# Gated cross-attention and low-rank expert layer on one core: turning tiles by VectorE blocks and SBUF moves in place of TensorE transposes

## The chip, the cores and the metric

One core of one Trainium2 chip runs the whole layer in one launch. The metric is the device time of that launch in microseconds (us), lower is better. Engine names as in the profile: PE is TensorE, DVE VectorE, ACT ScalarE, POOL GpSimd, SP SyncE (here it only waits and issues DMAs).

## The reference, cut to what matters

```python
# x, ctx: (16, 128, 1024) f32; attention: 8 heads of 64 over 128 channels; experts: 64 of rank 16, top 16
def xattn(q, k, v, Wq, Wk, Wv, Wo, bo, g):
    qh = einsum('bcn,oc->bon', q, Wq)            # likewise kh, vh, split into heads
    qh = softmax(qh, axis=-2) * SCALE            # over the 64 channels of a head
    kh = softmax(kh, axis=-1)                    # over the 1024 positions
    context = einsum('bhdn,bhen->bhde', kh, vh)
    out = einsum('bhde,bhdn->bhen', context, qh) # then Wo, + bo
    return out / norm(out, axis=1) * g * sqrt(128)
def ffn(x, A, B, Wr):
    scores = xf @ Wr.T                           # 64 scores a token, softmax over the top 16
    h = einsum('nd,krd->nkr', xf, A)             # 64 x 16 = 1024 hidden values a token
    return einsum('nkr,kdr->nd', h * G, B) * 2
x = x + tanh(g_xattn) * xattn(layernorm(x), ctx, ctx, ...)
x = x + tanh(g_ffn) * ffn(layernorm(x), A, B, Wr)
```

## The kernel before

**Arithmetic.** Every large product is made of three float32r passes (`three_pass`, lines 59 to 63): high part by high part, low by high, high by low. So each operand is kept as a pair: ACT copies it to float32r (the `hi_...` functions), and DVE or POOL subtracts that copy from the source (the `lo_...` functions).

**Stage one** (16 batch elements, bodies 0 to 15 and a tail body, `body(b, head, tail, ahead)` on each engine) is software-pipelined by hand: body b works on the keys and queries of element b and on the context and the output of element b-1. Keys: `mm_k(b, j)` makes key block j of four (128 key channels by 1024 positions) in the PSUM pair `psK`; DVE takes the maximum (`max_k`), ACT the exponential into `ek[:, j % 2]` (`exp_k`); PE turns it in eight 128x128 transposes into `psT` (`tr_k`, line 1298), ACT and DVE take the pair `ekT` from there (`hi_k` line 635, `lo_k` line 916). `psK` is single: `mm_k(b, j)` waits for `exp_k(b, j-1)`. `context(b)` (24 matmuls) needs all of `ekT` of element b, and runs at the start of body b+1. Queries go a similar way through `mm_q`, `max_q`, `shift_q` (subtracts the maximum by a matmul), `exp_q`, `tr_q` (line 1307), `hi_q`, `lo_q` and `output`. `psT` is handed from one turning to the next (`free_T`). DVE also has the layer norm of the next element (`stats`, `std`), and in bodies 2 to 4 one more reduction of 1024 elements, `part_early` (line 851). Each result of the attention goes to DRAM (`u_scratch`).

**Stage two** (`ffn_body`, b = 1 to 15): element b is normalised into `y` (the buffer `u_in`), turned by PE into `psY` (`tr_y`, line 1373, eight transposes), split by `hi_y` and `lo_y` into `yT`; `up(b, p)` multiplies by the router and A in three pieces (448, 384, 256 columns, 8 chunks of 3 passes each); DVE finds the top 16 (`route`) and gates the hidden values into `hg` (`gated`, line 1023); PE turns `hg` in two groups of four transposes (`tr_h`, line 1402), `hi_h` and `lo_h` split them into `hT`, and `down` multiplies by B (48 matmuls of 512 columns). DVE's `result` adds the residual. Beside that run the steps that prepare element b+2 and b+3: the load of u, `square_u`, `part_u`, `sum_u` (PE, line 1361), `norm_u` with `spread` (line 885), `residual` (POOL), `stats2`, `normalise`. The order on PE in a body:

```python
up(b, 0); tr_h(b - 1, 1); up(b, 1); up(b, 2); sum_u(b + 2)
tr_y(b + 1, j % 2); down(b - 1, 0); tr_h(b, 0); down(b - 1, 1)
```

What orders all this is the written order on each engine and the semaphores; nothing is planned by a scheduler. SP's order in a body of stage two is: store the result of b-2, load x of b+2, load u of b+3.

Of the kernel before, what the change touches and what calls it, by code (L numbers as in the profile page):

```python
# [6 lines left out]
def flamingo_layer(nc, x, ctx, ctxT, g_xattn, g_ffn, WqT, WkT, Wv, WoT, bo, g, AT, BT, u_dram, out):  # L7
# [9 lines left out]
    P = 128  # L17
# [70 lines left out]
    with outer:  # L88
# [8 lines left out]
        def at(kb, name, shape, dt=f32):  # L97
# [39 lines left out]
        ekT = [at(80, "ekT_hi", [P, BK, HD], f32r), at(96, "ekT_lo", [P, BK, HD], f32r)]  # L137
# [22 lines left out]
        yT = [at(152, "yT_hi", [P, DC, P], f32r), at(68, "yT_lo", [P, DC, P], f32r)]  # L160
        u_first = at(192, "u_first", [P, N])
# [7 lines left out]
        hT = [at(176, "hT_hi", [P, KC, P], f32r), at(180, "hT_lo", [P, KC, P], f32r)]  # L169
        hg = at(184, "hg", [P, KR])  # L170
# [12 lines left out]
        psN_early, psN = ps[:, 7, 0:EARLY * (N // 32)], ps[:, 4, 256:256 + N // 32]  # L183
# [14 lines left out]
            sem("k_mm"), sem("k_max"), sem("k_exp"), sem("k_T"), sem("k_hi"), sem("k_lo"), sem("k_rec"))  # L198
        q_mm, q_max, q_shift, q_exp, q_half, q_sum, q_rec, q_norm, q_T, q_hi, q_lo = (
# [50 lines left out]
        def _(sp):  # L250
# [52 lines left out]
            load_x(0, 0)  # L303
            sp.wait_ge(u_done, 1)
# [46 lines left out]
        def _(pool):  # L351
# [34 lines left out]

            def halve(b, p):
# [20 lines left out]
            def lo_a(t):  # L408
                pool.wait_ge(a_loaded, 16 * DC)
# [66 lines left out]
            def body(b, head, tail, ahead, split=False):  # L476
# [88 lines left out]
        def _(act):  # L565
# [32 lines left out]
            def exp_k(b, j):  # L598
# [977 lines left out]
```

## Time and profile before

| | |
|---|---|
| three runs | 959.32, 960.50, 960.53 us; median 960.5 |
| profiled execution | 959.67 us, of which its span is 957.9 us; granted TensorE clock 0.994 |
| PE | busy 932.2 us, 97% of the span, 5084 matmuls and transposes |
| PE weight load | busy 800.5 us |
| DVE, ACT, POOL | busy 704.0 (73%), 492.2 (51%), 469.5 us (49%) |
| chain that ended last | PE 81%, DVE 10%, issue 5% |
| stage one, stage two | to about 541 us; from about 550 us |

How to read it: the span is what the trace covers, and the rest of the execution (1.8 us) lies around it. Matmuls are pipelined, so a busy PE need not be PE at its peak: what one matmul costs is the distance of its start to the next start, which the chain that ended last gives. The share of a wait in that chain, not an engine's idle time, says what a shorter operation can give.

### The profile page before, as it was taken

The page shows a single profiled execution, that of the slowest core. Times are in us where ns is not written, and L with a number is a line of the kernel's source. Part 1 is how long each engine was busy: PE and PEld are TensorE (multiplying, and loading weights), DVE is VectorE, ACT ScalarE, POOL GpSimd, SP SyncE. Part 2 cuts the span into 40 slices and gives each one's busy share as a digit, 9 for nine tenths or more (in the row PEclk, how much of TensorE's full clock was granted, in tenths as well). Part 3 has the DMA queues.
Part 4 walks back from the last instruction along what each step waited for, and adds up shares of the span by engine and source line. Part 5 has one row for each costly group of instructions (what it writes and reads, how often), then busy time and mean ns, then how long its engine had stood idle before and what let it go on. Part 6 is the DMA issues. An engine that isn't in the chain of part 4 may idle for free.

```text
span 957.9 us, 16074 instructions
## 1 busy us (share of the span) xinstructions
PE 932.2 (97%) x5084; PEld 800.5 (84%) x5084; DVE 704.0 (73%) x1532; ACT 492.2 (51%) x974; POOL 469.5 (49%) x323
## 2 busy tenths in 40 slices
PE   7899999999999999999999799999999999999998
PEld 5687887888888888888888699999999999999986
DVE  6888888888888888888888857766666666666521
ACT  4687786678768767876787634222222222222100
POOL 3775657678777877785787824222222111111100
PEclk9999999999999999999999999999999999999999
DMA  4226231231323113311312853121111111111001
GB/s 153 89 66 249 93 104 49 89 133 66 109 91 133 66 68 132 109 68 66 131 45 88 300 199 128 67 67 67 66 67 67 66 66 66 66 66 45 23 23 44
DMA packets 24805, 88.31 MB, mean 92 GB/s; under 512 B 3264, under 2 KB 3264, under 8 KB 24768
## 3 DMA queue, kind: packets, MB, share of 16 engines
q1 hardware_dynamic: 19296, 67.91, 19.9%
q0 software_dynamic: 5184, 19.40, 6.1%
q10 hardware_dynamic: 288, 0.52, 0.2%
q8 instruction: 21, 0.34, 0.1%
q14 instruction: 16, 0.13, 0.0%
HBM read 71.04 MB, written 16.78 MB: 92 GB/s over the span
## 4 chain that ended last, share of the span: by engine, by line
PE 81%; DVE 10%; issue 5%; ACT 1%; POOL 1%; DMA 1%; DVEq 0%; ACTq 0%; POOLq 0%
PE ps L61 22%; PE ps L63 22%; PE ps L62 22%; PE ps L1307 6%; PE ps L1298 4%; DVE qT_lo L909 3%; PE ps L1288 2%; PE ps L1402 1%; PE ps L1373 1%; DVE mt L933 1%; DVE ekT_lo L916 1%; DVE qmax L895 1%; DVE bn L831 1%; DVE kmax L889 1%; DVE qsum L900 1%
## 5 line engine op out<-in xcount | busy, mean ns | idle before, releaser
L471 POOL TENSOR_TENSOR rb<-u_in,rb 128x1024 f32<-128x1024 f32 x14 | 33.7, 2408 | 255.4 <-DVE rb L885 255.4
L400 POOL TENSOR_TENSOR qe<-qe,qrec 128x1024 f32<-128x1024 f32 x64 | 121.2, 1903 | 47.1 <-DVE qrec L903 47.1
L61 PE MATMUL ps<-aT_hi,yT_hi 128*128 128x448 f32 (+2 forms) x384 | 128.4, 334 | 5.4 <-issue 5.4
L63 PE MATMUL ps<-aT_lo,yT_hi 128*128 128x448 f32 (+2 forms) x384 | 126.6, 330 | 0.0
L62 PE MATMUL ps<-aT_hi,yT_lo 128*128 128x448 f32 (+2 forms) x384 | 126.5, 330 | 0.0
L909 DVE TENSOR_TENSOR qT_lo<-ps,qT_hi 128x512 fp32r<-128x512 f32 x128 | 82.4, 686 | 49.0 <-ACT qT_hi L628 48.5
L393 POOL TENSOR_TENSOR qhalf<-qe 128x512 f32<-128x512 f32 x64 | 82.2, 1284 | 64.8 <-ACT qe L620 61.8
L61 PE MATMUL ps<-bT_hi,hT_hi 128*128 128x512 f32 x256 | 102.6, 401 | 0.0
L63 PE MATMUL ps<-bT_lo,hT_hi 128*128 128x512 f32 x256 | 100.0, 391 | 0.0
L62 PE MATMUL ps<-bT_hi,hT_lo 128*128 128x512 f32 x256 | 99.8, 390 | 0.0
L700 ACT ACTIVATE hT_hi<-ps 128x512 fp32r<-128x512 f32 x32 | 19.1, 597 | 143.8 <-PE ps L1402 143.8
L635 ACT ACTIVATE ekT_hi<-ps 128x512 fp32r<-128x512 f32 x128 | 70.1, 607 | 32.9 <-PE ps L1298 32.5
L916 DVE TENSOR_TENSOR ekT_lo<-ps,ekT_hi 128x512 fp32r<-128x512 f32 x128 | 81.2, 676 | 1.0 <-ACT ekT_hi L635 1.0
L889 DVE TENSOR_REDUCE kmax<-ps 128x1 f32<-128x1024 f32 x64 | 77.6, 1213 | 3.4 <-PE ps L63 1.9
L61 PEld LDWEIGHTS ps<-aT_hi,yT_hi 128*128 128x128 f32 x384 | 73.1, 190 | 8.0 <-issue 5.6
L604 ACT ACTIVATE ek<-ps,kmax 128x1024 f32<-128x1024 f32 x64 | 72.3, 1130 | 13.4 <-DVE kmax L889 13.4
L628 ACT ACTIVATE qT_hi<-ps 128x512 fp32r<-128x512 f32 x128 | 69.5, 599 | 14.4 <-PE ps L1307 14.4
L62 PEld LDWEIGHTS ps<-aT_hi,yT_lo 128*128 128x128 f32 x384 | 73.2, 191 | 2.3
L63 PEld LDWEIGHTS ps<-aT_lo,yT_hi 128*128 128x128 f32 x384 | 73.0, 190 | 2.0
L613 ACT ACTIVATE qe<-ps 128x1024 f32<-128x1024 f32 x48 | 49.3, 1027 | 47.8 <-PE ps L1288 47.7
L1307 PEld LDWEIGHTS ps<-ident,qe 128*128 128x128 f32 x512 | 57.9, 140 | 17.7 <-issue 8.5
L1307 PE MATMUL ps<-ident,qe 128*128 128x128 f32 x512 | 68.8, 276 | 3.8 <-DVE ekT_lo L916 3.5
(155 smaller groups left out, 2397.5 us busy)
## 6 DMA issues: line engine op xcount, KB each, us to landing
x_in<-in_x SPq DMA_DIRECT2D x16, 512.0 KB, 4.4
ctx_in<-in_ctx SPq DMA_DIRECT2D x16, 512.0 KB, 4.9
ctxT_in<-in_ctxT SPq DMA_DIRECT2D x16, 512.0 KB, 3.4
ctxT_hi<-in_ctxT POOLq DMA_DIRECT2D x16, 512.0 KB, 3.8
u_scratch<-osb SPq DMA_DIRECT2D x16, 512.0 KB, 3.8
out<-res SPq DMA_DIRECT2D x16, 512.0 KB, 2.8
x<-in_x SPq DMA_DIRECT2D x15, 512.0 KB, 4.0
u_in<-u_scratch SPq DMA_DIRECT2D x14, 512.0 KB, 3.2
```

What stands on the lines that cost most here:

```text
L61: nc.tensor.matmul(psum, whi, mhi, start=start, stop=False)
L62: nc.tensor.matmul(psum, wlo, mhi, start=False, stop=False)
L63: return nc.tensor.matmul(psum, whi, mlo, start=False, stop=stop)
L393: nc.gpsimd.tensor_tensor(qhalf[:, p % 2, :].rearrange("p (h d) -> p h d", d=DH // 2), v[:, :, 0:DH // 2], v[:, :, DH // 2:DH], ALU.add).t ...
L400: nc.gpsimd.tensor_tensor(v, v, w, ALU.mult).then_inc(q_norm, 1)
L604: nc.scalar.activation(ek[:, j % 2, :].rearrange("p (a n) -> p a n", a=HF), psK, ACT.Exp, bias=kmax[:, j:j + 1], accum_out=ksum[:, j:j + 1 ...
L628: nc.scalar.activation(qT[0][:, :, n * P:n * P + P], psT[:, h, :].rearrange("p (j n) -> p j n", n=P), ACT.Copy).then_inc(q_hi, 1)
L635: nc.scalar.activation(ekT[0][:, 4 * h:4 * h + 4, j * P:j * P + P], psT[:, h, :].rearrange("p (n d) -> p n d", d=P), ACT.Copy).then_inc(k_ ...
L889: nc.vector.tensor_reduce(kmax[:, j:j + 1], psK, axis=AX.XY, op=ALU.max, negate=True).then_inc(k_max, 1)
L909: nc.vector.tensor_tensor(qT[1][:, :, v], psT[:, h, :].rearrange("p (j n) -> p j n", n=P), qT[0][:, :, v].bitcast(f32), ALU.subtract).then ...
L916: nc.vector.tensor_tensor(ekT[1][:, n, w], psT[:, h, :].rearrange("p (n d) -> p n d", d=P), ekT[0][:, n, w].bitcast(f32), ALU.subtract).th ...
L1307: last = nc.tensor.transpose(psT[:, h, j * P:j * P + P], qe[:, p, w:w + P], ident[:, :])
```

## The change

Three of the turnings lose their TensorE transposes: those of `y` for elements 2 to 15, those of `hg` for all elements, and those of key block 0 of stage one. In their place DVE transposes the tile in place in blocks of 32x32 (`turn_y`, `turn_h`, `turn_k`), and SP moves the blocks between partition groups with 16 DMAs of 32 partitions by 256 columns each (32 KB) from SBUF to SBUF (`move_turned`). ACT and DVE (for keys ACT and POOL, `lo_moved_k`) then split the moved tile as a whole, 1024 columns at a time, from SBUF and not from PSUM. Key block 0 is moved into `ekT_raw[0]`, which lies on the low half of `ekT`, so its move waits for the context of the element before. The rows of A and B are laid out in another order on the host, to fit the order in which the strips land. `down` is one run of 48 matmuls. TensorE still turns key blocks 1 to 3, all of the queries, and `y` of elements 0 and 1.

```diff
+        MOVED = 16 * (P // 32) ** 2
+        def move_turned(queue, dst, src, s, slot=None):
+            for a in range(P // 32):
+                for q in range(P // 32):
+                    rows, cols = slice(32 * a, 32 * a + 32), slice(256 * q, 256 * q + 256)
+                    queue.dma_start(dst[32 * q:32 * q + 32, 256 * a:256 * a + 256],
+                                    src[rows, cols] if slot is None else src[rows, slot, cols]).then_inc(s, 16)
...
@@ SP @@
+            def move_k(b, j):
+                if j == 0 and started(b):
+                    wait_apart(sp, sp_turns, (kc_mm, b))
+                wait_apart(sp, sp_turns, (k_turned, turned_before(b, j) + 1))
+                move_turned(sp, ekT_raw[j], ek, k_moved[j], j % 2)
...
                     load(ctx_in[:, :], ctx, b + 1, ctx_loaded)
+                    for j in TURNED:
+                        move_k(b, j)
...
+            sp.wait_ge(h_turned, 1)
+            sp.wait_ge(o_mm, 2 * NB)
+            move_turned(sp, h_raw, hg, h_moved)
             def ffn_body(i, j):
...
+                if not isinstance(i, int) or b <= NB - 2:
+                    sp.wait_ge(y_turned, b)
+                    move_turned(sp, y_raw, y[(j + 2) % 2], y_moved)
                 if not isinstance(i, int) or b <= NB - 4:
-                    sp.wait_ge(y_T, 2 * b + 4)
+                    sp.wait_ge(y_moved, MOVED * b)
                     load_u(b + 3, j % 2)
+                sp.wait_ge(h_turned, b + 1)
+                move_turned(sp, h_raw, hg, h_moved)
@@ POOL, body @@
+            def lo_moved_k(b, j):
+                pool.wait_ge(k_hi, 8 * b + 2 * j + 2)
+                hi, lo = (t[:, 4 * j:4 * j + 4, :, :].rearrange("p g n i -> p (g n i)") for t in ekT)
+                nc.gpsimd.tensor_tensor(lo, ekT_raw[j][:, :], hi.bitcast(f32), ALU.subtract).then_inc(k_lo_pool, 1)
...
+                if head:
+                    lo_moved_k(b, 0)
                 if isinstance(b, int) and b == NB - 2:
                     early_newton()
@@ ACT, body @@
                 if head:
-                    hi_k(b, 0)
+                    hi_moved_k(b, 0)
+                if tail and head:
+                    hi_q(b - 1, 2)
+                if head:
                     exp_k(b, 2)
                     exp_q(b, 1)
-                if tail and head:
-                    hi_q(b - 1, 2)
@@ ACT, ffn_body @@
+                if not first:
+                    hi_moved_h(b - 1)
                 if not isinstance(i, int) or b <= NB - 2:
                     normalise(b + 1, (j + 2) % SLOTS)
-                hi_h(b - 1, 1)
+                if first:
+                    hi_moved_h(0)
                 exp_scores(b)
                 if not isinstance(i, int) or b <= NB - 2:
-                    hi_y(b + 1)
-                hi_h(b, 0)
+                    hi_moved_y(b + 1)
@@ DVE, body @@
                 if tail:
                     sum_q(b - 1, 2)
+                if head:
+                    turn_k(b, 0)
...
                     max_q(b, 1)
                     max_k(b, 2)
-                    lo_k(b, 0)
@@ DVE, ffn_body @@
+                if not first:
                     result(b - 2, (j + 1) % 2, (j + 3) % SLOTS, 2 * i + (j - 1) // 2)
-                if not isinstance(i, int) or b <= NB - 3:
+                    lo_moved_h(b - 1)
+                if norms:
                     part_u(b + 2)
+                if ahead:
+                    turn_y(b + 1, j % 2)
                 route(b)
-                if isinstance(i, int) and b == 1:
+                if first:
                     lo_b(4)
                     lo_b(6)
-                lo_h(b - 1, 1)
+                    lo_moved_h(0)
+                elif norms:
                     norm_u(b + 2)
                 for p in range(len(PIECES)):
                     gated(b, p)
-                    lo_y(b + 1)
-                lo_h(b, 0)
-                if not isinstance(i, int) or b <= NB - 3:
+                turn_h(b)
+                if ahead:
+                    lo_moved_y(b + 1)
+                if norms:
                     stats2(b + 2, (j + 3) % SLOTS)
@@ PE, body @@
                     mm_q(b, 1)
                     mm_k(b, 2)
-                    tr_k(b, 0, next(turn))
                 if tail and head:
+                    tr_q(b - 1, 2, next(turn))
                     output(b - 1, 0, range(CH // 2))
@@ PE, ffn_body @@
                 up(b, 0)
-                if isinstance(i, int) and b == 1:
-                    tr_h(0, 0)
-                else:
-                    tr_h(b - 1, 1)
+                if norms and not first:
+                    sum_u(b + 2)
                 up(b, 1)
                 up(b, 2)
-                    tr_y(b + 1, j % 2)
-                down(b - 1, 0)
-                tr_h(b, 0)
-                down(b - 1, 1)
+                down(b - 1)
```

`gated` now waits for the move of `hg` (`h_moved`) where it waited for `tr_h`, and `hi_moved_y` for the end of `up(b, 2)`, since `yT` is single. `context` waits for three blocks from DVE and one from POOL.

The order on SP's queue in one body of the loop of stage two, before (lines of the kernel before):

```order
L328 DMA out<-res_109 128x1024
L252 ISA
L252 DMA x_3_105<-in_x 128x1024
L333 REGISTER_ALU
L252 ISA
L252 DMA u_in_100<-u_scratch 128x1024
```

and with the change (lines of the changed kernel):

```order
L377 DMA out<-res_114 128x1024
L286 ISA
L286 DMA x_3_110<-in_x 128x1024
L250 DMA y_raw<-u_in_105 32x256 x16
L385 REGISTER_ALU
L286 ISA
L286 DMA u_in_105<-u_scratch 128x1024
L387 REGISTER_ALU
L250 DMA h_raw<-hg 32x256 x16
```

Three DMAs a body have become 35, and the load of u stands between the two moves. On DVE's queue, at the start of a body of stage one's loop, before (`qsum` is `sum_q`, `bn` the layer norm of the next element):

```order
L900 TENSOR_REDUCE qsum<-qhalf 128x16
L903 RECIPROCAL qrec<-qsum 128x16
L829 ISA
L831 BN_STATS bn<-x_in 128x6 x2
```

and with the change:

```order
L995 TENSOR_REDUCE qsum<-qhalf 128x16
L998 RECIPROCAL qrec<-qsum 128x16
L1015 ISA
L1016 STREAM_TRANSPOSE ek<-ek 128x1024
L924 ISA
L926 BN_STATS bn<-x_in 128x6 x2
```

The block turn stands ahead of the layer norm and of `max_q(b, 0)`; the two `ekT_lo` of block 0 further down are gone.

## Rows read from the trace of the kernel before

**Rows 1.** Chain that ended last in time order, stage two: start us, us, what.

```profile
700.93 0.44 PE ps L1402 x4
708.55 0.91 PE ps L1373 x8
709.46 0.23 PE ps L61
```

**Rows 2.** The same chain in stage one.

```profile
292.76 0.87 PE ps L1298 x8
```

**Rows 3.** Timeline of SP's queue, stage two: start us, us, line, operation.

```profile
709.64 0.33 SPq L252 DMA_DIRECT2D u_in<-u_scratch  x1
...
734.41 0.33 SPq L252 DMA_DIRECT2D u_in<-u_scratch  x1
```

**Rows 4.** Timeline of ACT, line 641 (once a body) in stage one.

```profile
111.28 0.60 ACT L641 ACTIVATE kc_hi<-ps 128x512 fp32r<-128x512 f32 x1 [0.66 <-PE ps L63]
...
145.06 0.60 ACT L641 ACTIVATE kc_hi<-ps 128x512 fp32r<-128x512 f32 x1 [0.65 <-PE ps L63]
...
310.29 0.60 ACT L641 ACTIVATE kc_hi<-ps 128x512 fp32r<-128x512 f32 x1 [1.20 <-PE ps L63]
...
343.17 0.60 ACT L641 ACTIVATE kc_hi<-ps 128x512 fp32r<-128x512 f32 x1 [1.21 <-PE ps L63]
```

**Rows 5.** Timeline of SP's queue between the stages.

```profile
542.90 0.33 SPq L252 DMA_DIRECT2D u_in<-u_scratch  x1
543.28 1.84 SPq L313 DMA_DIRECT2D b_raw<-in_BT  x4
```

**Rows 6.** Page, parts 3 and 6: q1 is SP's queue; last column us to landing.

```profile
q1 hardware_dynamic: 19296, 67.91, 19.9%
...
ctx_in<-in_ctx SPq DMA_DIRECT2D x16, 512.0 KB, 4.9
...
out<-res SPq DMA_DIRECT2D x16, 512.0 KB, 2.8
```

**Rows 7.** Groups by line and shape, DVE: busy us, mean ns of one.

```profile
L885 DVE STREAM_TRANSPOSE rb<-nr 128x1024 f32<-128x1024 f32 x14 | 17.4, 1245 | 0.8
...
L940 DVE TENSOR_TENSOR bT_lo<-b_raw,bT_hi 128x1024 fp32r<-128x1024 f32 x5 | 5.9, 1220 | 0.6 <-ACT bT_hi L661 0.6
```

**Rows 8.** Groups by line and shape, ACT.

```profile
L678 ACT ACTIVATE usq<-u_in 128x1024 f32<-128x1024 f32 x13 | 13.7, 1052 | 0.0
```

**Rows 9.** Timeline of DVE, one body of stage one.

```profile
310.07 0.69 DVE L900 TENSOR_REDUCE qsum<-qhalf 128x16 f32<-128x512 f32 x1 [0.53 <-POOL qhalf L393]
```

**Rows 10.** Timeline of ACT and PE, the same body.

```profile
321.00 1.11 ACT L604 ACTIVATE ek<-ps,kmax 128x1024 f32<-128x1024 f32 x1 [0.75 <-DVE kmax L889]
...
322.63 0.48 PE L61 MATMUL ps<-ctx_hi,wk_hi 128*128 128x512 f32 x1
```

**Rows 11.** Groups by line and shape, POOL.

```profile
L377 POOL TENSOR_TENSOR ctxT_lo<-ctxT_in,ctxT_hi 128x1024 fp32r<-128x1024 f32 x16 | 38.2, 2389 | 3.2 <-DMA ctxT_hi<-in_ctxT 3.2
```

**Rows 12.** Timeline of DVE and PE, the first body of stage one.

```profile
18.92 0.21 DVE L84 TENSOR_SCALAR rstd<-std_t,rstd 128x1 f32<-128x1 f32 x1
...
24.09 0.50 PE L61 MATMUL ps<-ctx_hi,wk_hi 128*128 128x512 f32 x1
```

**Rows 13.** Timeline of DVE, one body of stage two.

```profile
725.74 0.23 DVE L976 COPY sc<-ps 128x64 f32<-128x64 f32 x1 [1.78 <-PE ps L63]
...
728.95 0.69 DVE L1039 TENSOR_TENSOR hT_lo<-ps,hT_hi 128x512 fp32r<-128x512 f32 x1
733.37 0.19 DVE L862 TENSOR_SCALAR ns<-ps 128x32 f32<-128x32 f32 x1 [3.73 <-PE ps L1361]
...
738.25 1.27 DVE L1034 TENSOR_TENSOR yT_lo<-ps,yT_hi 128x512 fp32r<-128x512 f32 x2
```

**Rows 14.** Timeline of DVE and PE, first body of stage two's loop.

```profile
586.27 2.36 DVE L940 TENSOR_TENSOR bT_lo<-b_raw,bT_hi 128x1024 fp32r<-128x1024 f32 x2
...
585.35 0.47 PE L61 MATMUL ps<-bT_hi,hT_hi 128*128 128x512 f32 x1
```

More of the change, by code:

```diff
@@ L293, in _ @@
             sp.wait_ge(wq_low, 1)
-            for t in range(DC):
-                sp.dma_start(a_raw[:, t, :], AT[t]).then_inc(a_loaded, 16)
-            with sp.Fori(2, NB - 2) as b:
+            with sp.Fori(2, 2 + DC) as b:
+                sp.dma_start(a_raw[:, bass.ds(b - 2, 1), :].rearrange("p o n -> p (o n)"),
+                             AT[bass.ds(b - 2, 1)].rearrange("o p n -> (o p) n")).then_inc(a_loaded, 16)
+                body(b, head=True, tail=True, ahead=True)
+            with sp.Fori(2 + DC, NB - 2) as b:
                 body(b, head=True, tail=True, ahead=True)
@@ L696, in hi_y, with hi_moved_y, hi_moved_h @@
                                          ACT.Copy).then_inc(y_hi, 1)
-            def hi_h(b, g):
-                act.wait_ge(h_T, 2 * b + g + 1)
-                nc.scalar.activation(hT[0][:, 4 * g:4 * g + 4, :], psG.rearrange("p (n c) -> p n c", c=P),
-                                     ACT.Copy).then_inc(h_hi, 1)
+            def hi_moved_y(b):
+                act.wait_ge(h_mm, 3 * b)
+                act.wait_ge(y_moved, MOVED * (b - 1))
+                nc.scalar.activation(by_group(yT[0]), by_strip(y_raw), ACT.Copy).then_inc(y_hi, 2)
+            def hi_moved_h(b):
+                last = isinstance(b, int) and b == NB - 1
+                if last:
+                    act.wait_ge(h_mm, 3 * NB)
+                elif started(b):
+                    act.wait_ge(f_mm, 2 * b)
+                act.wait_ge(h_moved, MOVED * (b + 1))
+                nc.scalar.activation(by_group((hT_last if last else hT)[0]), by_strip(h_raw),
+                                     ACT.Copy).then_inc(h_hi, 2)
             def exp_scores(b):
@@ L1190, in _ @@
             gated(0, 2)
+            turn_h(0)
             lo_y(1)
@@ L1392, in up @@
                 last.then_inc(h_mm, 1)
-            def tr_h(b, g):
-                pe.wait_ge(hg_done, 3 * b + 2 + g)
-                if g == 1 or started(b):
-                    pe.wait_ge(h_lo, 2 * b + g)
-                else:
-                    pe.wait_ge(o_out, 2 * NB)
-                for n in range(4):
-                    w = (4 * g + n) * P
-                    last = nc.tensor.transpose(psG[:, n * P:n * P + P], hg[:, w:w + P], ident[:, :])
-                last.then_inc(h_T, 1)
@@ L1405, in down @@
[L1405 to L1419 removed]
+            def down(b):
+                hi, lo = hT_last if isinstance(b, int) and b == NB - 1 else hT
+                first = isinstance(b, int) and b == 0
+                pe.wait_ge(h_lo, 2 * b + 2)
+                for strips in (range(KC // 2), range(KC // 2, KC)) if first else (range(KC),):
+                    for g in range(2):
+                        if first:
+                            pe.wait_ge(o_out, 2 * NB)
+                        else:
+                            pe.wait_ge(res_done, 2 * b - 2 + g + 1)
+                        v = slice(512 * g, 512 * g + 512)
+                        for m in strips:
+                            if first and g == 0:
+                                wait_weight(pe, m)
+                            last = three_pass(psF[:, g, :], hi[:, m, :], lo[:, m, :], bT[0][:, m, v],
+                                              bT[1][:, m, v], m == 0, m == KC - 1)
+                        if strips[-1] == KC - 1:
+                            last.then_inc(f_mm, 1)
@@ L1458, in body @@
                         up(0, 0)
-                    tr_q(b - 1, 2, next(turn))
-                    if not head:
+                        tr_q(b - 1, 2, next(turn))
                         output(b - 1, 0, range(CH))
@@ L1550, in folded, with strips @@
         return w.reshape(-1, p, w.shape[1]).transpose(1, 0, 2).reshape(p, -1)
+    def strips(w):
+        return w.reshape(p // 32, -1, 32, w.shape[1]).transpose(1, 0, 2, 3).reshape(-1, p, w.shape[1])
     laid = {
```

154 lines of the change are left out of this document (91 added, 63 removed).

## The prediction

> **What bounds the kernel now.** I read the page first: PE is busy for 97% of the span, and most of the chain that ended last is PE. Busy time of a pipelined engine doesn't say what a transpose costs, so I took that from the chain in time order, where each piece is the distance to the next: four transposes of `hg` cost 0.44 us, eight of `y` 0.91, one matmul of 512 columns 0.23 [rows 1], eight of `ek` 0.87 [rows 2]. Then I looked for what else sits close behind PE. In stage two nothing does: a body lasts 734.41 - 709.64 = 24.77 us [rows 3], and two groups of `hg` and one of `y` make 0.44 x 2 + 0.91 = 1.79 of it, so PE alone would need 22.98. Stage one is another matter. Line 641 comes once a body: its bodies last 343.17 - 310.29 = 32.88 us, but 145.06 - 111.28 = 33.78 in bodies 2 to 4, which differ by one DVE reduction, `part_early` [rows 4]. It stands ahead of `max_q(b, 0)`, just where the change puts `turn_k`. So DVE work at that point costs nearly its full length, though DVE is not the busiest engine.
>
> **The price of a move.** No row shows a transfer within SBUF, or sixteen in a row. The nearest issues are four loads in 1.84 us, 0.46 each, and two at 542.90 and 543.28, 0.38 apart [rows 5]. For the landing: q1's packets took 19.9% of 16 engines' 957.9 us, over 19296 packets 0.158 us each; a 512 KB transfer has 144 of them (128 rows and 16 semaphore writes), 9 an engine, 1.4 us. A store lands 2.8 us after its issue, so 1.4 of that is fixed; the load of ctx 4.9, so 3.5 with others beside it [rows 6]. A move needs little time for its data (48 packets each), so it takes 15 distances and one fixed part: between 15 x 0.38 + 1.4 = 7.1 and 15 x 0.46 + 3.5 = 10.4 us. I take 0.46, since sixteen in a row are more like four than like two, and 1.9, nearer to the store, whose data also comes from SBUF: 8.8 us.
>
> The rest of the new work: a block turn 1.25 us, a subtraction of 1024 columns on DVE 1.22 [rows 7], a copy of 1024 on ACT 1.05 [rows 8].
>
> **Stage one, what goes.** Eight transposes of `ek` in each of 16 bodies: 16 x 0.87 = -13.9 us.
>
> **Stage one, an ordinary body.** Two routes lead from the end of `context(b-1)` (310.25, just before line 641 starts at 310.29) to `mm_k(b, 3)`, which needs `exp_k(b, 2)`. By DVE: `turn_k` adds 1.25 ahead of `sum_q(b-1, 3)`, where DVE sat idle for 0.53 [rows 9], so all behind it is 0.72 late. DVE stays busy without a gap from there through the matmul fold's `mt`, `lo_q(b-1, 1)`, `max_q(b, 1)` and `max_k(b, 2)`, so `exp_k(b, 2)` starts at 321.00 + 0.72 and, lasting 1.11 and 0.2 for its sum, ends near 323.0; `mm_k(b, 3)` began at 322.63 [rows 10]. By SP: 310.25 + 8.8 + the ACT copy 1.05 + about 1 for `hi_q(b-1, 2)` + `exp_k` 1.3 = 322.4. So DVE's route decides, and the segment gets 0.35 longer, not 0.87 shorter. `lo_k(b, 0)` is gone only behind that point, where DVE isn't on the path. POOL gets one subtraction of 2.39 us [rows 11] ahead of `normalise(b, 0)` and `lo_ctx(b+1)`, which `mm_k(b+1, 0)` awaits; in the eight bodies that also have `lo_a` this may show, for which I add 0.15 a body, an allowance. Cost against the gross saving: 13 bodies x (0.87 + 0.35 + 0.15) = +17.8. Bounds: 13 x 0.4 (the turn quite hidden, PE not held up) to 13 x 2.3 (moves of 10.4 us, 1.2 more on SP's route).
>
> **Stage one, its ends.** In body 0 nothing overlaps the move. DVE reaches `turn_k` at 18.92 + 0.3, so the move starts at 20.5, lands at 29.3, and copy and exponential end at 31.7; `mm_k(0, 3)` could have started at 24.09 - 0.87 [rows 12]. That is +8.5, of which later idle takes back 0.5: +8 (6 to 10 by the bounds of the move). In body 14 POOL has `early_newton`, without a gap from there to `lo_xn`, so the 2.39 goes through; with the steady cost of two bodies: 2 x 1.37 + 2.8 = +5.5. Sum for stage one: -13.9 + 17.8 + 8 + 5.5 = **+17.4**.
>
> **Stage two, what goes.** All 32 groups of `hg` and 14 of the 16 groups of eight of `y`: 32 x 0.44 + 14 x 0.91 = -26.8 us.
>
> **Stage two, an ordinary body.** Two new loops close once a body. (1) Through SP: move of `y` 8.8, load of u 0.4 (SP waits for the first move before it), move of `hg` 8.8, ACT copy 1.05, subtraction 1.22, `part_u` 1.2, `turn_y` 1.25: 22.7, and some eight hand-overs, for which I allow 0.05 each: 23.1. (2) Through DVE: move of `hg` 8.8, copy, subtraction, `part_u`, `turn_y` 4.7, `route` 728.95 - 725.74 = 3.2, `norm_u` with spread and the three gatings 738.25 - 733.37 = 4.9 [rows 13], `turn_h` 1.25: 22.9 and 0.3 for hand-overs, 23.2. PE needs 22.98. The three are level. With the load of u and the stores riding on the same queue I take 23.15: 13 bodies x 0.17 = +2. The lengths bind differently: PE's falls no lower, but each us more on a move adds 2 us a body in loop (1). The two-move loop is where a wait can take the place of the one removed: the first to show it would be `sum_u`, which needs `part_u`.
>
> **Stage two, its ends.** `lo_moved_h(0)` stands on DVE behind `lo_b(4)` and `lo_b(6)`, which ended at 586.27 + 2.36, and behind the two new turns: 588.6 + 2.5 + 1.2 = 592. `down(0)` began at 585.35, and would begin at 583.6 without the 1.79 of transposes ahead of it [rows 14]: +8 (5, if the turns fill idle time, to 11). At the end PE has only `down(14)`, 48 x 0.23 = 10.9 us, to cover 0.5 + 1.25 + 8.8 + 1.05 + 1.22 = 12.8: +2. Sum for stage two: -26.8 + 2 + 8 + 2 = **-14.8**.
>
> **The sum.** 17.4 - 14.8 = +2.6 on the profiled execution's 959.7 gives 962.3. The median of the runs, 960.5, is 0.8 above that execution, so **963 us**. Differences under 0.2%, 1.9 us, can't be told from none.
>
> **The skill against it.** The four loads above are all the trace has [rows 5]. The Trainium skill, DMA: Bandwidth & Descriptors, Rules for kernel authors, speaks against such a change: a transfer under 64 KB pays mostly overhead and should be joined with others; its section Anatomy of one DMA fits a fixed part of about 2.0 us (for GpSimd's path). By that, an estimate, a move would be 9.4 us and the sum about 14 us higher. No run here shows it yet.
>
> **The rivals.**
> - *Forecast, 0.40*: moves of 8.3 to 9.2 us, DVE's route decides in stage one, three level loops in stage two: 958 to 968, 963 likeliest.
> - *Short moves, 0.30*: issues 0.38 apart, as the pair [rows 5], and a landing of 1.4. Then the ends shrink by 1.7 each at three places, the 2 us of loops go, and if DVE catches up in stage one (it also loses the two subtractions of `lo_k(b, 0)`, about as much as a turn adds), `mm_k(b, 3)` is not late: another -5. -5 - 2 - 5 = -12: 951. For it: a move has a third of the packets of a load, so the queue may take it faster. Against it: `part_early` cost 0.9 of its 1.25.
> - *SP's loop becomes the bound, 0.25*: from a move of 9.3 us on, loop (1) is longer than loop (2) and PE. At 9.4, 24.3 a body: 13 x 1.15 = +15, 978. At 10.4, 26.3: 13 x 3.15 = +41 and 12 in stage one, over 1010. For it: the load of ctx with its 3.5, and two loads and a store a body in front of the moves. Against it: the store's 1.4. Slower by over 1%.
> - *Strided reading, 0.05*: `context` now reads its moving operand in 16 runs of 32 values 1 KB apart. No row has that. At 0.02 us more for each of 384 matmuls: +8, 971.
>
> **How the numbers follow.** Faster by over 0.2%: 0.28 of the short moves' 0.30 and 0.04 of the forecast's case, 0.32. Within 0.2% (958.6 to 962.4): 0.02 and 0.13, 0.15. Slower: 0.23 of the forecast's case, SP's loop and the strided reading, 0.53. The range, 947 to 992, takes in the short moves, the forecast and SP's loop up to moves of 9.7 us; the forecast's own range is 958 to 968.
>
> **What the changed profile would show.** Right: sixteen issues of SP in about 7.4 us, landing within 2 us after the last; stage-one bodies of 33.2 to 33.4, stage-two bodies of 23.0 to 23.3; PE waiting in `mm_k` for `exp_k` in each body of stage one (8 us once in body 0), and in `down(0)` for `hT_lo`. Wrong: a move of under 7.5 or over 9.3 us; `sum_u` or `down` waiting in every body; matmuls of `context` further apart than 0.23; a granted clock that falls in the new gaps.

## The result, and the profile after

The changed kernel took 1086.1 us (median of 4 runs, 1084.4 to 1088.4) against 960.5, a ratio of 1.131 (95% interval 1.129 to 1.133). The forecast was 963, 3 us slower, with a range of 947 to 992: it did come out slower, but by 126 us and far outside the range. The profiled execution is 1084.4 us, its span 1082.8.

Page after, parts 1, 2 and 4: busy time by engine, the granted clock in 40 slices, and the chain that ended last by engine.

```profile
span 1082.8 us, 16138 instructions
...
PE 945.9 (87%) x4716; PEld 799.8 (74%) x4716; DVE 733.2 (68%) x1516; ACT 492.1 (45%) x928; POOL 507.7 (47%) x339
...
PEclk9799999999999999999998998988998899989998
...
SPq 37%; PE 34%; DMA 8%; issue 8%; DVE 6%; ACT 5%; POOL 1%; ACTq 0%; DVEq 0%
SPq L250 37%; PE ps L71 9%; PE ps L73 9%; PE ps L72 9%; PE ps L1416 4%; PE ps L1425 3%; DMA h_raw<-hg 3%; DMA ekT_raw<-ek 3%; DMA y_raw<-u_in 2%; ACT ek L678 2%; ACT hT_hi L792 1%; DVE u_in L1138 1%; ACT qT_hi L701 1%; PE ps L1406 1%; DVE part L1170 1%
```

TensorE was 81% of that chain and is 34%. Its place is taken by SP's queue at line 250, the DMA of `move_turned`: 37%. No computing engine is the new bound (DVE was 10% of that chain and is 6%); the queue that issues the moves is.

The critical chain in time order, the end of one move of `hg` and what follows (start us, us, what), and then part 6 of the page (KB each, us to landing):

```profile
929.55 0.59 SPq L250
930.18 0.59 SPq L250
930.82 0.59 SPq L250
931.45 1.83 DMA h_raw<-hg
933.37 1.07 ACT hT_hi L792
```

```profile
ekT_raw<-ek SPq DMA_DIRECT2D x256, 32.0 KB, 1.9
...
h_raw<-hg SPq DMA_DIRECT2D x256, 32.0 KB, 1.8
```

Issues stand 0.63 us apart, where the loads of [rows 5] stood 0.46, and the last lands 1.8 later. A move is 15 x 0.63 + 1.8 = 11.3 us.

Timeline of SP's queue in stage two (a sixteenfold issue is one row):

```profile
921.64 0.33 SPq L286 DMA_DIRECT2D u_in<-u_scratch  x1
922.02 10.02 SPq L250 DMA_DIRECT2D h_raw<-hg  x16
932.30 0.37 SPq L377 DMA_DIRECT2D out<-res  x1
932.77 0.38 SPq L286 DMA_DIRECT2D x<-in_x  x1
938.06 10.09 SPq L250 DMA_DIRECT2D y_raw<-u_in  x16
949.58 0.34 SPq L286 DMA_DIRECT2D u_in<-u_scratch  x1
```

Against [rows 3]: this body is 949.58 - 921.64 = 27.94 us; from the load of u in body 1 to the one in body 12 the eleven distances are 27.9 to 30.0, 28.7 on average, where they were 24.8. SP issues moves for 20 of the 28. What TensorE waits for between 560 us and the end is what the prediction named as the first sign, `sum_u` for `part_u` (us in total, times, longest):

```profile
PE ps L1480 <- DVE part L1170: 39.4, 12, 5.0
```

For stage one, ACT at line 719 (it was 641), once a body, and PE where it waits; PE's waits for that releaser between 100 and 600 us stand last (engine, line, waited for: us in total, times, longest):

```profile
422.10 0.60 ACT L719 ACTIVATE kc_hi<-ps 128x512 fp32r<-128x512 f32 x1 [1.43 <-PE ps L73]
...
457.59 0.60 ACT L719 ACTIVATE kc_hi<-ps 128x512 fp32r<-128x512 f32 x1 [1.40 <-PE ps L73]
```

```profile
436.81 0.50 PE L71 MATMUL ps<-ctx_hi,wk_hi 128*128 128x512 f32 x1 [3.35 <-ACT ek L678]
```

```profile
PE ps L71 <- ACT ek L678: 41.6, 14, 4.0
```

Against [rows 4]: this body lasts 35.49 us; of the eight ordinary ones (bodies 5 to 12) two last 35.5 and six 37.1 or more; it was 32.88. In each, PE waits some 3.35 us in `mm_k(b, 3)` for `exp_k(b, 2)`.

The copies of `kc` cut every trace into three: up to the first, from there to the last (15 bodies of stage one), and the rest. The three parts are of the profiled execution. This table is used below; after_big4 and dram_noturn compute with wrongly placed values.

| us | to the first | 15 bodies | rest | all, median | ratio to before (95%) |
|---|---|---|---|---|---|
| before | 44.6 | 496.5 | 416.8 | 960.5 | |
| after | 55.9 | 554.3 | 472.6 | 1086.1 | 1.131 (1.129 to 1.133) |
| s2_only | 44.0 | 499.6 | 476.0 | 1019.9 | 1.061 (1.059 to 1.063) |
| after_fill | 55.5 | 542.4 | 477.0 | 1077.4 | 1.122 (1.120 to 1.124) |
| s2_split | 43.9 | 499.1 | 403.3 | 950.9 | 0.991 (0.989 to 0.992) |
| s2_hsplit | 44.5 | 499.3 | 456.1 | 1002.6 | 1.045 (1.041 to 1.048) |
| s2_hsplit2 | 44.0 | 499.6 | 444.3 | 989.6 | 1.031 (1.029 to 1.033) |
| s2_dram | 45.0 | 499.6 | 404.4 | 950.7 | 0.990 (0.988 to 0.991) |
| s2_dram_flat | 43.8 | 496.9 | 405.1 | 948.0 | 0.988 (0.987 to 0.990) |
| s2_dram_best | 44.1 | 496.7 | 412.2 | 955.3 | 0.996 (0.994 to 0.997) |
| s2_dram_best2 | 44.6 | 497.1 | 402.4 | 945.6 | 0.986 (0.984 to 0.988) |
| after_dram | 51.3 | 502.7 | 407.2 | 962.8 | 1.004 (1.002 to 1.005) |
| dram_noturn | 51.4 | 497.2 | 407.9 | 958.8 | 0.999 (0.998 to 1.000) |
| after_big4 | 46.4 | 501.1 | 405.1 | 954.2, one run | |

### The profile page after: what moved, and what is told of

Read it like the earlier page. It is cut to its first block, busy times and chain, and to the rows that moved or that the text cites. A ratio compares the mean times of both kernels' runs of the same rounds, so it can differ in the third digit from the quotient of the medians.

```text
span 1082.8 us, 16138 instructions
## 1 busy us (share of the span) xinstructions
PE 945.9 (87%) x4716; PEld 799.8 (74%) x4716; DVE 733.2 (68%) x1516; ACT 492.1 (45%) x928; POOL 507.7 (47%) x339
## 4 chain that ended last, share of the span: by engine, by line
SPq 37%; PE 34%; DMA 8%; issue 8%; DVE 6%; ACT 5%; POOL 1%; ACTq 0%; DVEq 0%
SPq L250 37%; PE ps L71 9%; PE ps L73 9%; PE ps L72 9%; PE ps L1416 4%; PE ps L1425 3%; DMA h_raw<-hg 3%; DMA ekT_raw<-ek 3%; DMA y_raw<-u_in 2%; ACT ek L678 2%; ACT hT_hi L792 1%; DVE u_in L1138 1%; ACT qT_hi L701 1%; PE ps L1406 1%; DVE part L1170 1%
## 5 line engine op out<-in xcount | busy, mean ns | idle before, releaser
L71 PE MATMUL ps<-aT_hi,yT_hi 128*128 128x448 f32 (+2 forms) x384 | 136.4, 355 | 2.9 <-issue 2.9
L72 PE MATMUL ps<-aT_hi,yT_lo 128*128 128x448 f32 (+2 forms) x384 | 134.3, 350 | 0.0
L73 PE MATMUL ps<-aT_lo,yT_hi 128*128 128x448 f32 (+2 forms) x384 | 133.9, 349 | 0.0
L459 POOL TENSOR_TENSOR qe<-qe,qrec 128x1024 f32<-128x1024 f32 x64 | 121.3, 1905 | 26.4 <-DVE qrec L998 26.4
L71 PE MATMUL ps<-ctx_hi,wk_hi 128*128 128x512 f32 x128 | 56.4, 441 | 59.5 <-ACT ek L678 56.1
L71 PE MATMUL ps<-bT_hi,hT_hi 128*128 128x512 f32 x240 | 94.9, 395 | 7.7 <-DVE hT_lo L1152 7.7
L71 PEld LDWEIGHTS ps<-aT_hi,yT_hi 128*128 128x128 f32 x384 | 79.7, 208 | 5.5 <-issue 3.0
L783 ACT ACTIVATE yT_hi<-y_raw 128x1024 fp32r<-128x1024 f32 x14 | 14.8, 1061 | 146.1 <-DMA y_raw<-u_in 146.1
L72 PEld LDWEIGHTS ps<-aT_hi,yT_lo 128*128 128x128 f32 x384 | 79.4, 207 | 2.3
L71 PEld LDWEIGHTS ps<-ctx_hi,wk_hi 128*128 128x128 f32 x128 | 25.4, 198 | 72.1 <-ACT ek L678 63.2
L708 ACT ACTIVATE ekT_hi<-ps 128x512 fp32r<-128x512 f32 x96 | 52.6, 605 | 35.8 <-PE ps L1416 35.4
```

The costliest lines, as they stand in the source:

```text
L71: nc.tensor.matmul(psum, whi, mhi, start=start, stop=False)
L72: nc.tensor.matmul(psum, wlo, mhi, start=False, stop=False)
L73: return nc.tensor.matmul(psum, whi, mlo, start=False, stop=stop)
L459: nc.gpsimd.tensor_tensor(v, v, w, ALU.mult).then_inc(q_norm, 1)
L708: nc.scalar.activation(ekT[0][:, 4 * j:4 * j + 4, 4 * h:4 * h + 4, :].rearrange("p g n i -> p n g i"), psT[:, h, :].rearrange("p (n g i) - ...
```

## Which stage costs what

**s2_only** undoes stage one's part:

```diff
-    TURNED = (0,)
-    KEPT = (1, 2, 3)
+    TURNED = ()
+    KEPT = (0, 1, 2, 3)
@@ PE, ACT, DVE: tr_k(b, 0), hi_k(b, 0), lo_k(b, 0) back in their places; move_k, turn_k, hi_moved_k, lo_moved_k gone @@
```

> Stage two as changed, stage one as before (TensorE turns all four key blocks; the new layout of ekT stays). Theory: the change's cost in stage one is (610.2 - 55.9) - (541.2 - 44.6) = 57.7 us over 15 bodies and 11.3 in body 0, by the copies of kc in the two traces; without it 1086 - 69 = 1017 us. Stage-one bodies of 32.9, stage-two bodies of 28 to 29. Rival: the strided reading of context, which stays, is part of the cost: bodies of 33.2 and 1021 us.

1019.9 us. So stage one's part is worth 66 of the 125.6 us. The other 59 lie in stage two, but for some 3 us by which stage one stays longer than before (499.6 against 496.5). The rival of this run holds: ordinary bodies last 33.17 us, not 32.88.

**after_fill** keeps TensorE busy in the new waits:

```diff
+            def fill(bank, n):
+                for k in range(n):
+                    nc.tensor.matmul(bank, ident_r[:, :], ident_r[:, :].unsqueeze(1).broadcast_to([P, 4, P]),
+                                     start=True, stop=True)
@@ body @@
+                if head and tail:
+                    fill(psX[:, 1, :], 12)
                 if head:
                     mm_k(b, 3)
@@ ffn_body @@
+                    fill(psG, 12)
                     sum_u(b + 2)
```

> The changed kernel with 12 idle matmuls of 512 columns (about 2.8 us) put into the wait ahead of mm_k(b, 3) in stage one and 12 ahead of sum_u in stage two; nothing reads what they write. Theory (clock): part of the loss is TensorE's granted clock, which falls in these waits (mean 0.95 to 0.97 in stage one); kept busy it stays up, stage-one bodies fall from 37.0 to about 35.6, and the time by 15 to 20 us, to 1066 to 1071. Rival: only the waits count; the idle matmuls hide in them and the time stays at 1086, or rises by what does not fit.

1077.4 us, 8.7 less: added work made it faster, by less than the 15 to 20 expected. By the table it is 11.9 less in the fifteen bodies of stage one and 4.4 more in the rest. In the changed kernel six of the eight ordinary bodies run at half the rate for about 3 us, soon after that wait: PE's timeline at 401 us, where starts of 512-column matmuls are 0.43 apart and not 0.23.

```profile
401.19 0.60 PE L71 MATMUL ps<-wq_hi,xn_hi 128*128 128x512 f32 x1
401.59 0.63 PE L72 MATMUL ps<-wq_hi,xn_lo 128*128 128x512 f32 x1
402.02 0.63 PE L73 MATMUL ps<-wq_lo,xn_hi 128*128 128x512 f32 x1
402.45 0.63 PE L71 MATMUL ps<-wq_hi,xn_hi 128*128 128x512 f32 x1
```

The granted clock from 402 to 404 us is 0.50, the lower level of 1.2 GHz; it was 1.00 up to 401, and before that TensorE had been idle for 3.36 us. Over a whole ordinary body it is 0.95 or less in those that last 37.1 or more, and 1.00 in the two of 35.5, whose idle stretches are as long (3.38 and 3.35); why it did not fall in these two the trace doesn't show. With the idle matmuls it is 1.00 in all eight, and all last 35.5 to 35.6; the three bodies with `part_early` (bodies 2 to 4) last 0.7 to 1.7 longer with them. So the clock is about 12 us of stage one's 66, and the wait and the start of body 0 most of the rest. In stage two TensorE isn't the bound, so a faster TensorE should give little there; that the idle matmuls get in the way where the wait is short is my reading of the 4.4 us, not shown.

## What makes a move long

**s2_split**: two queues issue each move; `move_h` and `move_y` are ACT's part, transfers 8 to 15 and 10 to 15.

```diff
-                    move_turned(sp, y_raw, y[(j + 2) % 2], y_moved)
+                    move_turned(sp, y_raw, y[(j + 2) % 2], y_moved, pieces=range(BY_ACT_Y[0]))
@@ ACT @@
+                    move_h(b - 1)
                     hi_moved_h(b - 1)
...
                 exp_scores(b)
+                    move_y(b + 1, (j + 2) % 2)
                     hi_moved_y(b + 1)
```

> As s2_only, and each move's sixteen transfers are issued by two queues: of h 8 by SP and 8 by ACT, of y 10 and 6. Theory: a move is long because of the 0.63 us between issues of one queue. Then a move of h takes 7 x 0.63 + 1.8 = 6.2 us, of y some 7.5, the loop through SP 19, and TensorE bounds stage two again at 23.0 us a body: about 15 x 1.8 = 27 below the kernel before and some 6 back at the two ends, 940 us. Rival: the two queues share what takes 0.63 us for one transfer; a move stays at 11.3 and the time at 1017 us.

950.9 us, 69 less than s2_only and 9.6 less than before, a gain of 1% that is clear of noise. It is 11 more than expected: bodies come to 23.0 as expected, but stage one keeps its 3 us of s2_only, and from 560 us on TensorE waits 10.6 us in four places, 7.7 of them in `down(0)`, against 6 expected. The timeline of ACT's and of SP's queue over the same move of `hg`, and then SP's and ACT's over a move of `y`:

```profile
693.09 1.30 ACTq L252 DMA_DIRECT2D h_raw<-hg  x2
...
694.42 3.82 ACTq L252 DMA_DIRECT2D h_raw<-hg  x6
```

```profile
690.38 4.97 SPq L252 DMA_DIRECT2D h_raw<-hg  x8
```

```profile
704.31 7.02 SPq L252 DMA_DIRECT2D y_raw<-u_in  x10
705.00 4.18 ACTq L252 DMA_DIRECT2D y_raw<-u_in  x6
```

In the move of `hg` the two queues overlap for 2 us, and each keeps a distance of 0.63 to 0.64. In the moves of `y` they overlap almost wholly, and the distances average 0.69 on SP and 0.70 on ACT, where one queue alone has 0.66 (y_raw in s2_only). So most of what takes 0.63 is not shared; a twentieth or so may be. The Trainium skill, DMA: Bandwidth & Descriptors, section Issuing engines are not separate DMA queues, says that several issuing engines save only the sequencer's time to initiate, "which is usually small relative to the DMA itself". That it saves this time agrees with this run; but here the time isn't small: fifteen distances of 0.63 are 9.5 of a move's 11.3 us.

**s2_dram** and **after_big4** lower the number of transfers. The first goes through HBM and reads four groups of rows back in the new order; the second copies 128 rows at once without regrouping them.

```diff
+            queue.dma_start(turn_dram[which], src).then_inc(turn_out[which], 16)
+            queue.wait_ge(turn_out[which], 16 * times)
+            for q in range(P // 32):
+                queue.dma_start(dst[32 * q:32 * q + 32, :].rearrange("r (a c) -> r a c", a=P // 32),
+                                turn_dram[which].rearrange("(a r) (q c) -> q r a c", r=32, c=256)[q]).then_inc(s, 16)
@@ after_big4 @@
+            for q in range(P // 32):
+                cols = slice(256 * q, 256 * q + 256)
+                queue.dma_start(dst[:, cols], src[:, cols] if slot is None else src[:, slot, cols]).then_inc(s, 16)
```

> As s2_only, but a move goes through HBM: one store of 512 KB, a wait for it on SP, and four loads of 32 partitions x 4 runs of 1 KB. Theory (number of issues): 2.8 for the store, 3 x 0.46 + 3.2 for the loads, 7.4 us a move; the loop through SP is 20.5, TensorE bounds stage two: about 942 us. Rival: rows of 1 KB scattered over HBM land in 5 us or more; a move is 9.3 or longer, the loop 24.3, 960 us or more.

> The changed kernel with each move as four transfers of 128 rows of 1 KB within SBUF, rows not regrouped (so what follows computes with wrongly placed values); bytes and rows are the same. Theory (a price for each transfer): 3 x 0.63 + 2 = 4 us a move, both stages as for a short move: about 958 us, stage-two bodies of 23.0. Rival (bytes or rows set the 0.63): the four transfers take as long as the sixteen, 11 us, and the time stays at 1086.

950.7 and 954.2 us. The first is 9 more than expected: stage one keeps its 3 us of s2_only, and TensorE waits 8.7 us in `down(0)`. The second is 4 less than expected. SP's timeline in stage two, of s2_dram_flat (which differs from s2_dram in stage one alone) and then of after_big4:

```profile
666.92 0.34 SPq L250 DMA_DIRECT2D turn_scratch<-hg  x1
669.71 1.74 SPq L253 DMA_DIRECT2D h_raw<-turn_scratch  x4
```

```profile
720.39 2.41 SPq L249 DMA_DIRECT2D h_raw<-hg  x4
```

The way through HBM takes 669.71 - 666.92 = 2.8 for the store, 1.3 for three distances of the loads (1.74 less the last issue's own 0.42) and 2.8 until the last lands (part 6 of its page), together 6.9 us, less than sixteen transfers within SBUF. In after_big4 each transfer has four times the rows and bytes, and they still stand about 0.6 apart (2.41 less one issue of 0.6, by three); the last lands after 2.1, so a move is some 3.9 us. So the distance goes by the transfer, not by its rows or bytes. It also differs by kind: 0.6 within SBUF in both shapes; 1.32 / 3 = 0.44 for these loads from HBM, and 0.47 for the four of [rows 5], whose shape is another (starts 543.28 to 544.69).

The Trainium skill's rule that I had weighed (same page, Rules for kernel authors: transfers under 64 KB are mostly overhead) agrees with the runs in its direction: four transfers of 128 KB take 3.9 us where sixteen of 32 KB take 11.3. Its bound of 64 KB is tested by no run here. The estimate that I had made from the Trainium skill, 9.4 us a move, was too low like my own, since it too stood on the distance of 0.46; and it counted sixteen distances where my sum has fifteen, with which it would have been 8.9.

**s2_hsplit** and **s2_hsplit2** split the move of `hg` alone, to see whether a microsecond of a move is a microsecond of the body.

```diff
@@ s2_hsplit2, ACT @@
-                    move_h(b - 1)
                     hi_moved_h(b - 1)
...
                 exp_scores(b)
+                move_h(b)
                 hi_moved_y(b + 1)
```

> s2_only with only the moves of h issued by two queues (8 transfers each); y stays with sixteen by SP. Theory (the loop through SP holds both moves, so a body changes by what one of them changes): a move of h falls from 11.3 to 6.2 us, the loop from 28.0 to 28.9 to 23.0 to 23.8, level with TensorE's 23.0: 13 bodies x 5 to 5.5 below s2_only, and 5 us less at each of the two ends: 942 to 955 us. Rival (each queue's moves count by themselves, or the granted clock holds TensorE up): the saving is half of that or less, 980 us or more.

> s2_hsplit with ACT's eight issues of the move of h put right behind exp_scores, ahead of hi_moved_y and square_u. In s2_hsplit they stood behind square_u, which waits for u, so ACT began them at 739.8, 5 us after the block turn of hg had ended (734.7) and 3.2 after SP's half (736.6): the body was y's move 12.7, load of u 3.6, ACT's issues 5.2, landing 1.4, copy to turn_y 4.7 = 27.6. Theory (whatever the sixteen and their order put on this loop counts in full): now 12.7 + 0.4 + SP's issues 5.0 + 1.8 + 4.7 = 24.6, so 13 x 2.8 less, 966 us. Rival (splitting h gives little in itself, the clock or another loop holds the body at 27): 1000 us.

1002.6 and 989.6 us: both far slower than the theories said (942 to 955, and 966); by the number alone s2_hsplit fits its rival, and s2_hsplit2 lies between the two. ACT's queue in s2_hsplit shows a reason:

```profile
739.77 1.06 ACT L755 ACTIVATE usq<-u_in 128x1024 f32<-128x1024 f32 x1 [2.60 <-DMA u_in<-u_scratch]
739.83 1.37 ACTq L252 DMA_DIRECT2D h_raw<-hg  x2
740.74 1.13 ACT L756 ACTIVATE u_in<-u_in,gcol 128x1024 f32<-128x1024 f32 x1
741.23 3.83 ACTq L252 DMA_DIRECT2D h_raw<-hg  x6
746.45 1.06 ACT L791 ACTIVATE hT_hi<-h_raw 128x1024 fp32r<-128x1024 f32 x1 [4.58 <-DMA h_raw<-hg]
```

ACT's half stood behind `square_u`, which waits for the load of u, and that for the whole move of `y`: 12.7 + 3.6 + 5.2 + 1.4 + 4.7 = 27.6, the measured body, and the mean of ten. With the issues ahead of it, the body shown is 25.8, not 24.6, and the mean of ten 26.4. SP's queue, and then ACT's:

```profile
721.46 10.92 SPq L252 DMA_DIRECT2D y_raw<-u_in  x16
733.84 0.34 SPq L288 DMA_DIRECT2D u_in<-u_scratch  x1
734.23 5.11 SPq L252 DMA_DIRECT2D h_raw<-hg  x8
...
747.22 10.65 SPq L252 DMA_DIRECT2D y_raw<-u_in  x16
```

```profile
730.81 5.07 ACTq L252 DMA_DIRECT2D h_raw<-hg  x8
736.07 1.06 ACT L782 ACTIVATE yT_hi<-y_raw 128x1024 fp32r<-128x1024 f32 x1 [13.57 <-issue]
```

From the copy of `hT` (740.66) to the next move of `y` it is now 6.6 us where it was 4.7: the issues hold ACT up ahead of `hi_moved_y`, DVE's `lo_moved_y`, `stats2` and `result` stand behind that, and `lo_moved_h` behind them. In this body the chain that ended last runs through ACT's eight issues and DVE, and not through SP. So the links of the loop add up to the body in both traces, but that is read after the fact, and one change moved two links: an issue that leaves SP's queue takes its 0.63 us from the engine that takes it.

## The strided reading, the first body, and stage one again

**s2_dram_flat** lays `ekT` out as before; **s2_dram_best** and **s2_dram_best2** also turn `h` of element 0 by TensorE.

```diff
@@ flat @@
-        ekT = [at(80, "ekT_hi", [P, HD // 32, BK, 32], f32r), at(96, "ekT_lo", [P, HD // 32, BK, 32], f32r)]
+        ekT = [at(80, "ekT_hi", [P, BK, HD], f32r), at(96, "ekT_lo", [P, BK, HD], f32r)]
@@ best: tr_h0, hi_h0, lo_h0 stand where tr_h(0, g), hi_h(0, g), lo_h(0, g) stood @@
+            nc.scalar.activation(h_raw[:, :].rearrange("c (m a i) -> c m a i", a=4, i=32),
+                                 hg[:, :].rearrange("c (a m i) -> c m a i", a=4, i=32), ACT.Copy).then_inc(h_perm, 1)
@@ best2, SP; on ACT the copy above stands ahead of hi_b(2) and hi_b(3) @@
-            sp.wait_ge(h_turned, 1)
```

> As s2_dram, with ekT laid out as in the kernel before, so that context reads 512 values in a row and not 16 runs of 32. Theory (strided reading): its matmuls were 0.237 apart, against 0.228 before; 384 of them give 3.3 us: 947.4 us. Rival: the distance comes from something else (the clock): no change from 950.7.

> As s2_dram_flat, and h of element 0 turned by TensorE (ACT first copies it into the order of the strips), since nothing covers its move: down(0) waited 8.7 us for hT_lo. Theory: that wait goes, less two groups of transposes, 0.9, and what the two weights lo_b(4), lo_b(6) still hold up: 4 to 7 us below s2_dram_flat, 941 to 943 us. Rival: DVE's lo_b and the gating of body 1 come next, and the wait only moves: 947.

> s2_dram_best with two things mended: SP no longer waits for the first block turn of hg (at 595 us) ahead of the first move of y, which it held back from 584 to 596.4 us; and ACT's copy of h of element 0 stands ahead of hi_b(2) and hi_b(3), for which TensorE waited 2.6 us. Theory: the 4.4 and 4.1 us that TensorE waited for yT_lo and for part in that body go, and the 8.7 of s2_dram_flat with them: 940 to 943 us. Rival: DVE's lo_b(4) and lo_b(6) ahead of lo_h0(1) still hold down(0) up, 3 to 5 us: 945 us.

Flat: 948.0 us, and the fifteen bodies of stage one go from 499.6 to 496.9: reading 16 runs of 32 values costs 0.27 us in an ordinary body. The 24 matmuls of `context` stand 0.237 apart in the changed kernel (5.2 us for 22 distances), and 0.228 before and in flat (5.0 us). Best: 955.3, slower, by a mistake of mine: a wait for the first block turn of `hg` was left on SP, and since element 0 no longer has one, the first move of `y` stood behind the turn of element 1. Without it, and with ACT's copy further forward, 945.6. The intervals of flat and best2 overlap, so best2's own gain of 2 us isn't certain; both beat the two kernels given. PE's waits between 560 and 700 us in best2, and DVE's rows in flat, where 8.7 were waited:

```profile
PE ps L71 <- DVE hT_lo L1132: 4.8, 1, 4.8
```

```profile
588.37 0.23 DVE L1070 TENSOR_TENSOR gsel<-gsel,ex 128x64 f32<-128x64 f32 x1 [4.78 <-ACT ex L774]
...
589.25 2.35 DVE L1011 TENSOR_TENSOR bT_lo<-b_raw,bT_hi 128x1024 fp32r<-128x1024 f32 x2
591.52 1.22 DVE L1124 TENSOR_TENSOR hT_lo<-h_raw,hT_hi 128x1024 fp32r<-128x1024 f32 x1
```

The wait in flat has two parts. DVE's `route(1)` stands idle for 4.78 us for `exp_scores(1)`, which on ACT comes behind `hi_moved_h(0)`, the copy of the moved `hg`; then come `lo_b(4)` and `lo_b(6)`. In best2, without the move, the second part is left, 4.8 us for `down(0)` and 945.6 in all: this is the rival of its expectation.

**after_dram** is the whole change with short moves, **dram_noturn** the same without DVE's turn of key block 0 (one block of 32x32 is turned instead of all).

```diff
@@ dram_noturn @@
-                nc.vector.transpose(ek[:, j % 2, :], ek[:, j % 2, :]).then_inc(k_turned, 1)
+                nc.vector.transpose(ek[0:32, j % 2, 0:32], ek[0:32, j % 2, 0:32]).then_inc(k_turned, 1)
```

> The whole change, stage one's part too, with all three moves through HBM (one store, four loads), which took 7.0 us in stage two. Theory: at 7 us the exponential of key block 2 waits for DVE's route and no more for the move, as the prediction had it at 8.8: stage-one bodies of 33.2 to 33.5, against 32.9 before and 37.0 changed, body 0 some 7 us longer than before; 951 + 14 x 0.4 + 7 = about 964 us. Rival (a turned block costs stage one nothing once its move is short): bodies of 32.3, 950 us.

> after_dram, and DVE's block turn of key block 0 reduced to one block of 32 x 32 (so the values of key block 0 are left unturned); everything else runs. Theory (the prediction's for stage one): DVE's route to exp_k(b, 2) decides, and the turn lies on it; without its 1.2 us the stage-one body falls from 32.87 by the 0.7 us that TensorE waits there, to 32.2: 962.8 - 13 x 0.7 = 954 us. Rival: another loop of the same length, which the turn isn't on, holds the body at 32.87: 962 us.

962.8 and 958.8 us. The second is 4 less; it fits neither the theory (954) nor the rival (962). The ordinary body of after_dram is 353.84 - 320.97 = 32.87, what it was before, and not the 33.2 to 33.5 expected, with 0.87 of transposes less:

```profile
320.97 0.60 ACT L722 ACTIVATE kc_hi<-ps 128x512 fp32r<-128x512 f32 x1 [1.42 <-PE ps L73]
...
331.81 1.11 ACT L681 ACTIVATE ek<-ps,kmax 128x1024 f32<-128x1024 f32 x1 [0.46 <-DVE kmax L987]
```

From `kc_hi` to `exp_k(b, 2)` it is 10.84 us; before it was 321.00 - 310.29 = 10.71 [rows 4, 10]; after_big4, with a move of 3.9, has 10.83; without the turn it is 10.74 in seven of the eight ordinary bodies (10.88 in one), and TensorE still waits 0.7 there. DVE ahead of `mt`, before and without the turn:

```profile
315.97 1.41 DVE L933 TENSOR_TENSOR mt<-ps,krec 64x512 f32<-64x512 f32 x2 [0.50 <-PE ps L63]
```

```profile
321.61 1.41 DVE L1035 TENSOR_TENSOR mt<-ps,krec 64x512 f32<-64x512 f32 x2 [0.50 <-PE ps L73]
```

In after_dram, with the turn, that wait is 0.61. So DVE is done with all that stands ahead of `mt`, the turn too, before PE's fold releases it; neither the move nor the turn sets the body, but PE's fold and DVE's work behind it (`mt`, `lo_q`, `max_q`, `max_k`), which the change leaves alone. TensorE just waits where the transposes used to be. The 4 us of dram_noturn lie elsewhere: the three bodies with `part_early` lose 1.0 to 2.7 us each, the ordinary ones 0.1.

## Why the prediction was wrong, step by step

- **What bounds**: right. TensorE in stage two, DVE close behind it in stage one.
- **The price of a move**: this step failed. The row taken was of loads from HBM, 0.46 apart [rows 5]; transfers within SBUF stand 0.63 apart. 15 x 0.63 + 1.8 = 11.3 against 8.8 forecast and 10.4 as the upper bound. The fixed part (1.9 forecast, 1.8 measured) and "little time for its data" were right: four times the bytes in a transfer left the distance at 0.6 and put 0.3 on the landing. Both ends of my bounds were distances of one kind of transfer, and I called them bounds for another.
- **Loop (1) in stage two**: right, with the wrong move in it. 23.1 + 2 x (11.3 - 8.8) = 28.1, where 27.9 to 30.0 were measured, 28.7 on average. That was the rival "SP's loop becomes the bound", which had 0.25 and stopped at 10.4. 13 x (28.1 - 22.98) = 67 in place of 2. With a move of 6.9 us (after_dram) the bodies last 23.1, as the sum had it for TensorE's bound.
- **Ends**: `down(0)` waited 7.7 (forecast 8), but the number is luck. The forecast added up DVE's own operations, up to `lo_b(4)` and `lo_b(6)` and the two turns, and gave the move no part in it; in the changed kernel, as in flat, `route(1)` stood idle for `exp_scores(1)` behind the copy of the moved `hg`, for 3.78 us. The last element waited 8.4, not 2: some 2.5 by the longer move, the rest mostly because `route(15)` begins on DVE only behind `lo_moved_h(14)`, so the block turn ended 4.7 us after `down(14)` had begun, and not 1.75. Body 0: 55.9 - 44.6 = 11.3, forecast 8 on top of a saving of 0.9; with a 7 us move, 6.7.
- **Stage one, ordinary body, SP's route**: 310.25 + 11.3 + 3.35 = 324.9, 2.3 behind [rows 10]; so 35.15, measured 35.5 at the full clock. I listed the falling clock only among the signs of being wrong and priced it at nothing; it added 1.6 us to five of eight ordinary bodies and 2.5 to one.
- **Stage one, DVE's route**: mis-sized and partly for a wrong reason. The turn's 0.72 was to go through "without a gap", which misread the trace of before: DVE has 0.50 us ahead of `mt`, in which it waits for PE. Of the turn 0.1 is left. That the 0.87 of transposes gives nothing there was right. In the three bodies with `part_early`, which the sum took for ordinary ones, the turn does cost 1.0 to 2.7.
- **Strided reading**: I gave it 0.05 and 8 us; it is there, and costs 3 us.
- After_dram lands on 963, but by terms that offset one another: its bodies of stage one cost 6 (4 in those with `part_early`, 2.3 in body 14, nothing in the ordinary ones) and body 0 cost 7, 13 in place of 17.4; the rest gave 9.6 in place of 14.8. It isn't a confirmation of the sum.

Not tried: why a transfer within SBUF costs SP 0.63 us; and stage one's part with a move short enough and its first body left to TensorE.

## What to carry to other kernels

Before work leaves the bounding engine for DMAs, count the issues, and price them by a row of the same kind (source, destination, back to back): an issue takes the time of its queue, and sixteen of them, 10 us here, keep everything behind them waiting. If no row has that kind, the bounds are wide, and a loop that holds it twice doubles the error; look then for a form with fewer transfers, such as a store and four loads through HBM. And an operation taken off an engine gives only what no second chain of the same length takes back: in the ordinary body of stage one that was nothing.

## What the runs showed of the hardware

- Transfers within SBUF: 0.63 us apart in one queue for 32 KB (0.63 to 0.72 over the moves of the changed kernel), and 0.60 for 128 KB; loads from HBM 0.44 to 0.47. With SP's and ACT's queue side by side 0.69 and 0.70 each, against 0.66 for one.
- 512 KB to HBM and back in four regrouped loads: 6.9 us. The first one of s2_dram_flat, beside four loads of 512 KB on POOL's queue, took 7.8 for its store alone.
- TensorE idle for 3.35 us once a body: in six of eight ordinary bodies it ran soon after at 1.2 GHz for some 3 us (granted clock 0.50), in two it did not; with twelve idle matmuls in the gap it stayed at 2.4 GHz in all eight.
- A moving operand in 16 runs of 32 values: matmuls of 512 columns 0.237 apart, against 0.228.
